# Order of the steps in the first pass of the second attention: variance before the score products on VectorE, ScalarE counted one tile later

## The chip, the cores and the metric

The kernel runs on one core of one Trainium2 chip. The metric is the device time of one execution in microseconds (us); the time of the kernel is the median of its runs.

## What is computed

The reference is four residual graph layers over 50000 nodes of 256 features and 12500 edges, each followed by a row norm. The change lies in the third layer, an attention with 8 heads over the edges, and there in what is computed per edge before the softmax:

```python
q = (nfeat @ Wq.T).reshape(n, HEADS, HEAD_DIM) / SCALING
k = (nfeat @ Wk.T).reshape(n, HEADS, HEAD_DIM)
v = (nfeat @ Wv.T).reshape(n, HEADS, HEAD_DIM)
attn = jnp.einsum('ehd,ehd->eh', k[src], q[dst]) + attn_bias
...
x = _layernorm(x + _L2_gnn_ref(...))
```

## The kernel before

The 12500 edges, sorted by destination, are 100 tiles of 125 edges. `attention_scores` (line 1864) is one pass over these tiles. It takes for each edge the row of its destination and the row of its source out of a table in HBM, brings the destination row to the norm that the layer before left open, projects both, and leaves two things in SBUF: V (the projected source row) and the score of each head. A barrier stands before the pass and after it; behind it come the maximum per destination and the sums.

Per tile, five queues work on it, each in an order that is written out by hand:

- POOL, `fetch`: two indirect gathers, the destination rows `xd` (a ring of 4 buffers) and the source rows `xs` (a ring of 8). It waits until ScalarE has normed the tile four earlier, whose `xd` buffer it fills again.
- VectorE: `stats` and `aggregate` (mean and variance of each row of `xd`), `variance` (two instructions on one column: `q`, line 1999, and `mean`, line 2001), `rest` (line 2006, the part of a transposed tile that rounding dropped), and `dots` (lines 2012 to 2014: product of k and q, sum per head, bias; after each of the three VectorE waits until it is done, and then counts `s_dot` up).
- ScalarE: `normed` (lines 1946 to 1951: logarithm, exponential, shift, and the normed rows `xn`), `copy_rows` (line 1957, the transposed tile out of PSUM, rounded), `copy_out` (lines 1963 and 1964: q scaled, and V, both out of PSUM).
- TensorE: `turn_rows` (line 1924, four transposes) and `project` (line 1935, 18 matmuls: q, k, v). A tile's `project` waits for its own `rest`, and, as its two PSUM buffers turn over, for `dots` and the copy of V two tiles earlier.
- SP: `keep` stores the normed rows.

The order on an engine is a list of (lag, step) pairs. `run_stages` (line 909) goes through the tiles t and runs, in the order of the list, each step on tile t - lag:

```python
for a in range(unroll):
    for lag, step in steps:
        step(At(turn, unroll, a - lag))
```

The first 16 passes and those behind pass 96 are written out with constant semaphore values (the head and the tail). The 80 passes between are a loop of eight passes per turn, in which semaphore values and addresses come from registers. Before, VectorE's list is `[(0, stats), (3, rest), (0, aggregate), (4, dots), (0, variance)]` and ScalarE's `[(0, normed), (1, copy_rows), (3, copy_out)]`. POOL has no loop: its 100 fetches are written out.

Of the kernel before, what the change touches and what calls it, by code (L numbers as in the profile page):

```python
# [36 lines left out]
T = E // P  # L37
# [39 lines left out]
class Chain:  # L77
# [5 lines left out]
    def step(self, ins):  # L83
        self.go(ins)
        self.done()
# [814 lines left out]
def wait(eng, sem, value):  # L900

    if not (isinstance(value, int) and value <= 0):
        eng.wait_ge(sem, value)
# [5 lines left out]
def run_stages(eng, steps, total, tiles=100, unroll=RING, behind=4):  # L909

    most = max(lag for lag, _ in steps)
    head = unroll * -(-(most + behind) // unroll)
    for t in range(head):
        for lag, step in steps:
            if 0 <= t - lag < total:
                step(At(0, unroll, t - lag))
    with eng.Fori(head // unroll, tiles // unroll) as turn:
# [3 lines that stand above are left out]
    for t in range(unroll * (tiles // unroll), total + most):  # L921
        for lag, step in steps:
            if 0 <= t - lag < total:
                step(At(0, unroll, t - lag))
# [939 lines left out]
def attention_scores(nc, env, V, score):  # L1864
# [10 lines left out]
    stages = dict(unroll=LONG, behind=LONG)  # L1875
# [11 lines left out]
    with nc.Block() as block:  # L1887
        @block.gpsimd
        def _(pool):
            dram = Rows(ph, pool, N)  # L1890
            pool.wait_ge(s_index, 4)

            def fetch(at):
                s, l = at.slot(RING), at.slot(LONG)
                wait(pool, s_st, at.count(1, 1 - RING))
                wait(pool, s_xn[s], at.uses(RING))
                wait(pool, s_t, at.count(1, 1 - LONG))
                dram.gather(xd[:, s, :], env["XX"], dst2[:, at.col], s_d[s])
                dram.gather(xs[:, l, :], env["XX"], src2[:, at.col], s_s[l])
            run_unrolled(pool, [(0, fetch)], T)  # L1900
# [39 lines left out]
        @block.scalar  # L1940
        def _(act):
            def normed(at):
                s = at.slot(RING)
                act.wait_ge(s_q, at.count(2, 2))
                ch = Chain(act, ca, at.count(3))
                ch.step(act.activation(lnq[:, s, :], q[:, s, :], ACT.Ln, bias=rec[:, at.col, 3]))
                ch.step(act.activation(c[:, s, :], lnq[:, s, :], ACT.Exp, scale=-0.5))
                ch.step(act.activation(nm[:, s, :], mean[:, s, :], ACT.Copy, scale=c[:, s, :]))
                wait(act, s_t, at.count(1, 1 - RING))
                wait(act, s_o[s], at.uses(RING, 32))  # L1950
                act.activation(xn[:, s, :], xd[:, s, :], ACT.Identity, bias=nm[:, s, :], scale=c[:, s, :]).then_inc(s_xn[s], 1)

            def copy_rows(at):
                s, b = at.slot(RING), at.slot(2)
                act.wait_ge(s_t, at.count(1, 1))
                wait(act, s_p, at.count(1, 1 - RING))
                act.copy(xT[:, s, 0, :, :], tp[:, b, :, 0:P]).then_inc(s_xT, 1)

            def copy_out(at):
                s, b = at.slot(RING), at.slot(2)  # L1960
                act.wait_ge(s_p, at.count(1, 1))
                wait(act, s_dot, at.count(1, 1 - RING))
                act.mul(qs[:, s, :], kq[:, b, F:2 * F], float(C2) ** 0.5).then_inc(s_qs, 1)
                act.copy(V[:, at.col, :].rearrange("p o f -> p (o f)"), vp[:, b, 0:F]).then_inc(s_V, 1)
            run_stages(act, [(0, normed), (1, copy_rows), (3, copy_out)], T, **stages)

        @block.vector
        def _(dve):
            dve.tensor_scalar(fresh[:, :], rec[:, :, 3], -1.0, 1.0, ALU.mult, ALU.add).then_inc(s_index, 1)
            dve.tensor_scalar(unfresh[:, :], rec[:, :, 3], 1.0, None, ALU.subtract).then_inc(s_index, 1)  # L1970
            dve.scalar_tensor_tensor(out=dst2[:, :], in0=rec[:, :, 3], scalar=float(N), in1=rec[:, :, 1],
                                     op0=ALU.mult, op1=ALU.add).then_inc(s_index, 1)
            dve.tensor_scalar(src2[:, :], rec[:, :, 0], float(N), None, ALU.add).then_inc(s_index, 1)
            dve.wait_ge(s_index, 2)
            weights = ((0, 2 * F, env["w_kv"]), (2 * F, 3 * F, env["w_q"]))
            for a, e, w in weights:
                dve.tensor_copy(wp[:, 0, :, a:e], w[:, :, :]).then_inc(s_wr, 1)
            dve.wait_ge(s_wr, 2)
            for a, e, w in weights:
                dve.tensor_tensor(wp[:, 1, :, a:e], w[:, :, :], wp[:, 0, :, a:e], ALU.subtract).then_inc(s_wp, 1)  # L1980

            def stats(at):
                s = at.slot(RING)
                dve.wait_ge(s_d[s], at.uses(RING, 16, 16))
                wait(dve, s_mv, at.count(1, 1 - RING))
                dve.bn_stats(st[:, s, :], xd[:, s, :]).then_inc(s_st, 1)

            def aggregate(at):
                s = at.slot(RING)
                wait(dve, s_q, at.count(2, 2 - 2 * RING))  # L1990
                dve.wait_ge(s_st, at.count(1, 1))
                dve.sem_inc(s_hold, 1)
                dve.bn_aggr(mv[:, s, :], st[:, s, :]).then_inc(s_mv, 1)

            def variance(at):
                s = at.slot(RING)
                dve.wait_ge(s_mv, at.count(1, 1))
                wait(dve, s_xn[s], at.uses(RING))
                dve.scalar_tensor_tensor(out=q[:, s, :], in0=mv[:, s, 1:2], scalar=EPS, in1=fresh[:, at.col],
                                         op0=ALU.add, op1=ALU.mult).then_inc(s_q, 1)  # L2000
                dve.tensor_scalar(mean[:, s, :], mv[:, s, 0:1], unfresh[:, at.col], None, ALU.mult).then_inc(s_q, 1)

            def rest(at):
                s, b = at.slot(RING), at.slot(2)
                dve.wait_ge(s_xT, at.count(1, 1))
                dve.tensor_tensor(xT[:, s, 1, :, :], tp[:, b, :, 0:P], xT[:, s, 0, :, :], ALU.subtract).then_inc(s_rest, 1)  # L2006

            def dots(at):
                s, b = at.slot(RING), at.slot(2)
                ch = Chain(dve, c1, at.count(3))  # L2010
                dve.wait_ge(s_qs, at.count(1, 1))
                ch.step(dve.tensor_tensor(prod[:, s, :], kq[:, b, 0:F], qs[:, s, :], ALU.mult))
                ch.step(dve.tensor_reduce(dot[:, s, :], prod[:, s, :].rearrange("p (h c) -> p h c", h=H2), X, ALU.add))
                ch.step(dve.tensor_tensor(score[:, at.col, :].rearrange("p o h -> p (o h)"), dot[:, s, :],
                                          rec[:, at.col, 4:4 + H2].rearrange("p o h -> p (o h)"), ALU.add))
                dve.sem_inc(s_dot, 1)
            run_stages(dve, [(0, stats), (3, rest), (0, aggregate), (4, dots), (0, variance)], T, **stages)
    ph.end()


# [515 lines left out]
```

## Time and profile before

| | us |
|---|---|
| median of 3 runs | 4572.68 |
| lowest and highest run | 4570.46, 4578.47 |
| the profiled execution, its own time | 4575.74 |
| its span in the trace | 4573.1 |
| first gather of the pass to the first instruction behind it | 3228.25 to 3673.60 |

The span is what the trace shows from the first to the last instruction. Over the whole program TensorE is busy for 75% of it, VectorE for 71%, POOL for 64% and ScalarE for 59%, but the program is a row of stages with a barrier between them, and a share over all of them tells nothing of one. The pass of this case is 445 us long, and it is read by itself: start times in a timeline are in us from the span's start, the second number is the duration in us, and what stands in square brackets at the end of a row is how long the engine was idle before it and which instruction ended that. A start that comes before the end of the row ahead on the same engine means that the two overlap.

### The profile page before, as it was taken

What the parts mean: (1) busy time and instruction counts of PE and PEld (TensorE: products, weight loads), DVE (VectorE), ACT (ScalarE), POOL (GpSimd) and SP (SyncE); (2) the same over time, 40 slices, a digit from 0 to 9 for tenths busy, and PEclk for the clock granted to TensorE, in tenths of its full rate; (3) what the DMA queues carried; (4) which work ended last, traced back from release to release, by engine and by line L of the source; (5) the groups of instructions that cost most, each with busy time, mean ns of one, the idle gap of its engine ahead of it and who ended that gap; (6) DMA issues with size and microseconds to landing.
All of it is one profiled execution on the core that took longest, in us unless ns stands there. A gap on an engine that the chain in (4) does not pass through costs nothing. (4 is left out here: it accounts for less than half of the span.)

```text
span 4573.1 us, 92084 instructions
## 1 busy us (share of the span) xinstructions
PE 3430.6 (75%) x17524; PEld 2595.8 (57%) x17524; DVE 3237.9 (71%) x11747; ACT 2715.4 (59%) x6436; POOL 2914.7 (64%) x2826
## 2 busy tenths in 40 slices
PE   4899934445999997999999777777566658850588
PEld 2799922223888886666666555555466635530365
DVE  7788843334555556999999798999555587740798
ACT  0688812222666666989989588888555536640366
POOL 0366658885434443888888788887655537667476
PEclk9999955555999998999999787777799979985799
DMA  1688823332444446888888333333333337753344
GB/s 54 177 237 236 238 74 80 79 80 79 162 161 161 161 161 185 269 268 267 264 265 267 104 99 99 98 100 97 98 88 88 86 95 213 214 161 82 97 135 115
DMA packets 437548, 685.41 MB, mean 150 GB/s; under 512 B 171062, under 2 KB 284588, under 8 KB 437396
## 3 DMA queue, kind: packets, MB, share of 16 engines
q1 hardware_dynamic: 263572, 521.77, 37.2%
q0 software_dynamic: 173824, 162.17, 14.7%
q14 instruction: 124, 1.02, 0.1%
q8 instruction: 28, 0.46, 0.0%
HBM read 352.28 MB, written 339.16 MB: 151 GB/s over the span
## 5 line engine op out<-in xcount | busy, mean ns | idle before, releaser
L1097 POOL TENSOR_TENSOR mlp_r_parts<-mlp_r,mlp_r_parts 128x500 fp32r<-128x500 f32 x200 | 253.0, 1265 | 403.4 <-ACT mlp_r_parts L1083 394.3
L1238 PE MATMUL nodes_xp<-w_self,nodes_x3T 128*125 128x256 f32 x1600 | 444.0, 400 | 45.5 <-DVE nodes_elu L1346 45.5
L791 PE MATMUL gram<-gin_both,gin_am 125*128 125x257 f32 x404 | 205.8, 665 | 266.8 <-DVE gin_both L774 254.6
L1238 PEld LDWEIGHTS nodes_xp<-w_self,nodes_x3T 128*125 128x125 f32 x1600 | 268.3, 187 | 111.3 <-ACT nodes_x3T L1277 39.0
L791 PEld LDWEIGHTS gram<-gin_both,gin_am 125*128 125x128 f32 x404 | 118.1, 322 | 354.4 <-issue 323.2
L1122 DVE BATCH_NORM_STATS2 mlp_stats<-mlp_y 128x500 f32 (+1 forms) x200 | 136.3, 682 | 253.3 <-ACT mlp_y L1073 253.3
L179 POOL DMA_INDIRECT by_src<-rank_recs,rank_place x100 | 119.7, 1197 | 293.2 <-DVE rank_recs L512 292.6
L1392 POOL TENSOR_TENSOR nodes_v<-nodes_elu,nodes_x 125x512 f32<-125x512 f32 x200 | 253.4, 1267 | 79.1 <-ACT nodes_x L1270 44.6
L1036 PE MATMUL mlp_y<-mlp_hT,mlp_w 128*128 128x500 f32 x1200 | 296.6, 396 | 1.5 <-DVE mlp_hT L1113 0.8
L1036 PE MATMUL mlp_y<-mlp_r_parts,mlp_w 128*128 128x500 f32 x1200 | 287.4, 388 | 0.8 <-ACT mlp_y L1073 0.8
L572 PE MATMUL gram<-rank_xc 125*128 125x257 f32 (+1 forms) x1600 | 279.1, 328 | 0.0
L1935 PE MATMUL att_kq<-att_w_parts,att_xT 128*125 128x256 f32 x1200 | 176.0, 298 | 136.6 <-DVE att_xT L2006 136.6
L572 PEld LDWEIGHTS gram<-rank_xc 125*128 125x128 f32 x1600 | 249.2, 191 | 22.4
L1081 ACT ACTIVATE mlp_r<-mlp_y,affine 128x500 f32<-128x500 f32 x200 | 153.7, 768 | 178.9 <-PE mlp_y L1036 178.9
L1036 PEld LDWEIGHTS mlp_y<-mlp_r_parts,mlp_w 128*128 128x128 f32 x1200 | 225.3, 188 | 47.1 <-POOL mlp_r_parts L1097 1.1
L744 DVE SCALAR_TENSOR_TENSOR gin_acc<-gin_acc,same,gin_msg 125x256 f32<-125x256 f32 x100 | 48.4, 484 | 286.6 <-ACT gin_msg L716 205.7
L1384 POOL TENSOR_SCALAR nodes_x<-nodes_u,nodes_r,nodes_nm 125x256 f32<-125x256 f32 x400 | 217.7, 553 | 45.7 <-DVE nodes_nm L1339 33.9
L1935 PEld LDWEIGHTS att_kq<-att_w_parts,att_xT 128*125 128x125 f32 x1200 | 154.7, 194 | 158.8 <-DVE att_xT L2006 138.6
L1036 PEld LDWEIGHTS mlp_y<-mlp_hT,mlp_w 128*128 128x128 f32 x1200 | 218.1, 188 | 41.0 <-DVE mlp_hT L1116 1.1
L716 ACT ACTIVATE gin_msg<-gin_xd,srec 125x256 f32<-125x256 f32 x100 | 50.7, 507 | 316.0 <-DMA gin_xd<-x,other 316.0
L1251 ACT ACTIVATE nodes_z<-nodes_y,affine 128x250 f32<-128x250 f32 x400 | 215.2, 588 | 33.3 <-ACT nodes_r L801 18.0
L175 POOL DMA_INDIRECT att_xd<-XX,att_dst x100 | 121.4, 1214 | 159.0 <-issue 150.5
(426 smaller groups left out, 11951.3 us busy)
## 6 DMA issues: line engine op xcount, KB each, us to landing
XX<-mlp_y SPq DMA_DIRECT2D x100, 500.0 KB
nodes_y<-XX SPq DMA_DIRECT2D x100, 500.0 KB
rank_xin<-x SPq DMA_DIRECT2D x100, 448.0 KB
XP<-rank_xc SPq DMA_DIRECT2D x100, 448.0 KB
mlp_h<-XP SPq DMA_DIRECT2D x100, 448.0 KB
nodes_x<-x SPq DMA_DIRECT2D x100, 448.0 KB
XX<-nodes_x SPq DMA_DIRECT2D x100, 448.0 KB
out<-nodes_out SPq DMA_DIRECT2D x100, 448.0 KB
```

Source lines behind the costliest of these rows:

```text
L175: self.pool.indirect_dma_start(out, None, table, bass.IndirectOffsetOnAxis(index, 0)).then_inc(sem, 16)
L572: mm = pe.matmul(gram[:, m, 128 * m:F + 1], xc[:, s, j, 128 * m:128 * m + 128], xc[:, s, j, 128 * m:F + 1], start=False, stop=True, skip_g ...
L791: mm = pe.matmul(gram[:, m, 0:F + 1], am[:, s, 128 * m:128 * m + 128], both[:, s, 0:F + 1], start=False, stop=True, skip_group_check=True)
L1036: mm = pe.matmul(out[:, m, 0:CH], w[:, a, k, 128 * m:128 * m + 128], rows[:, s, b, k, :], start=((k, a, b) == terms[0]), stop=((k, a, b) = ...
L1081: act.activation(r[:, s, m, :], y1[:, m, 0:CH], ACT.Relu, bias=aff[:, 1, m:m + 1], scale=aff[:, 0, m:m + 1]).then_inc(s_r, 1)
L1097: pool.tensor_tensor(rp[:, s, 1, m, :], r[:, s, m, :], rp[:, s, 0, m, :], ALU.subtract).then_inc(s_rp, 1)
L1122: dve.bn_stats(stats[:, m, at.col, :].rearrange("p o n -> p (o n)"), y[:, s, m, :]).then_inc(s_st, 1)
L1238: pe.matmul(xp[:, b, j, :], x3T[:, s, k, P * j:P * j + P], w_self[:, k, 0:F], start=(k == 0), stop=False)
L1251: act.activation(z[:, s, m, :], y[:, c, m, HC * h:HC * h + HC], ACT.Relu, bias=aff[:, 3, m:m + 1], scale=aff[:, 2, m:m + 1]).then_inc(s_z, 1)
L1384: pool.tensor_scalar(x1[:, s, j, :], u[:, at.slot(LONG), j, :], r[:, s, 0, j:j + 1], nm[:, s, 0, j:j + 1], ALU.mult, ALU.add).then_inc(s_x ...
L1392: pool.tensor_tensor(v[:, at.slot(LONG), :, :], el[:, s, :, :], x3[:, at.slot(LONG), :, :], ALU.add).then_inc(s_v, 1)
L1935: mm = pe.matmul(out, xT[:, s, i, x0 + k, :], wp[:, j, k, w0:w0 + F], start=((k, i, j) == terms[0]), stop=((k, i, j) == terms[-1]), skip_g ...
```

## The change

```diff
@@ attention_scores, block.scalar
-            run_stages(act, [(0, normed), (1, copy_rows), (3, copy_out)], T, **stages)
+            run_stages(act, [(1, normed), (2, copy_rows), (4, copy_out)], T, **stages)
@@ attention_scores, block.vector
-            run_stages(dve, [(0, stats), (3, rest), (0, aggregate), (4, dots), (0, variance)], T, **stages)
+            run_stages(dve, [(0, stats), (3, rest), (0, aggregate), (0, variance), (5, dots)], T, **stages)
```

On VectorE, pass t now does `variance` of tile t right behind `aggregate` of tile t, and only then `dots`, of tile t - 5 in place of t - 4. On ScalarE all three lags are one higher. No instruction is added, removed or changed in shape; PE, POOL and SP have the same rows in the same order.

VectorE in the loop, from `rest` on, in the kernel before (q and mean are `variance`, prod, dot and score are `dots`; ISA and REGISTER_ALU rows are waits and register work between the instructions):

```order
L2006 TENSOR_TENSOR att_xT<-att_tp,att_xT 128x500
L1991 REGISTER_ALU
L1993 BN_AGGR att_mv<-att_stats 125x2
L2012 TENSOR_TENSOR att_prod<-att_kq,att_qs 125x256
L93 REGISTER_ALU
L2013 TENSOR_REDUCE att_dot<-att_prod 125x8
L93 REGISTER_ALU
L2014 ISA
L2014 REGISTER_ALU
L2014 TENSOR_TENSOR att_score<-att_dot,srec 125x8
L1999 ISA
L1999 SCALAR_TENSOR_TENSOR att_q<-att_mv,att_fresh 125x1
```

and the same place in the kernel with the change:

```order
L2006 TENSOR_TENSOR att_xT<-att_tp,att_xT 128x500
L1991 REGISTER_ALU
L1993 BN_AGGR att_mv<-att_stats 125x2
L1999 ISA
L1999 SCALAR_TENSOR_TENSOR att_q<-att_mv,att_fresh 125x1
L2001 REGISTER_ALU
L2001 TENSOR_SCALAR att_mean<-att_mv,att_unfresh 125x1
L2012 TENSOR_TENSOR att_prod<-att_kq,att_qs 125x256
L93 REGISTER_ALU
L2013 TENSOR_REDUCE att_dot<-att_prod 125x8
L93 REGISTER_ALU
L2014 ISA
```

`variance` has moved from behind `dots` to ahead of it; what stands behind the score's row there (not shown) is the next pass's `stats`.

ScalarE just ahead of the loop's branch (line 917), one piece of the difference:

```order
 L1963 ACTIVATE att_qs<-att_kq 125x256
 L1964 COPY att_v<-att_vp 125x256
-L1946 ACTIVATE att_lnq<-att_q,srec 125x1
-L1947 ACTIVATE att_c<-att_lnq 125x1
-L1948 ACTIVATE att_nm<-att_mean,att_c 125x1
-L1951 ACTIVATE att_xn<-att_xd,att_nm,att_c 125x256
-L1957 CAST att_xT<-att_tp 128x500
-L1963 ACTIVATE att_qs<-att_kq 125x256
-L1964 COPY att_v<-att_vp 125x256
 L917 UNCONDITIONAL_BRANCH
```

The same seven rows stand behind the loop's end in the kernel with the change. Since all three lags rise by the same one, the order of ScalarE's work by tiles (`normed` of tile m, `copy_rows` of m - 1, `copy_out` of m - 3) is the order of before, and only the place where head, loop and tail are cut has moved by one tile.

## Rows read from the trace of the kernel before

**Rows 1.** Windows: stretch, length; PE, PEld, DVE, ACT, POOL busy us (instructions); PEclk, DMA, GB/s.

```profile
3256.50:3295.40 38.90, 28.09 (x221) 25.77 (x220) 23.03 (x81) 23.97 (x71) 24.23 (x20) 1.00 0.40 100
3297.00:3650.00 353.00, 237.72 (x1758) 220.15 (x1759) 188.66 (x640) 192.00 (x560) 193.54 (x160) 0.96 0.34 88
2540.00:2900.00 360.00, 263.78 (x1071) 185.88 (x1070) 307.16 (x1371) 262.51 (x763) 286.79 (x246) 0.78 0.37 98
3243.10:3247.00 3.90, 3.88 (x18) 3.88 (x19) 1.43 (x6) 1.39 (x4) 2.99 (x4) 0.50 0.46 119
```

**Rows 2.** Waits from 3260 to 3660: engine, line, releaser: total us, times, longest.

```profile
ACT att_lnq L1946 <- DVE att_mean L2001: 168.1, 92, 2.0
```

**Rows 3.** Timeline, one tile in the loop, DVE, ACT and POOL.

```profile
3451.79 0.18 DVE L1999 SCALAR_TENSOR_TENSOR att_q<-att_mv,att_fresh 125x1 f32<-125x1 f32 x1 [0.33 <-DVE att_score L2014]
3451.90 0.21 DVE L2001 TENSOR_SCALAR att_mean<-att_mv,att_unfresh 125x1 f32<-125x1 f32 x1
...
3452.27 0.29 ACT L1946 ACTIVATE att_lnq<-att_q,srec 125x1 f32<-125x1 f32 x1 [1.89 <-DVE att_mean L2001]
...
3453.16 0.60 ACT L1951 ACTIVATE att_xn<-att_xd,att_nm,att_c 125x256 f32<-125x256 f32 x1
3453.67 0.55 ACT L1957 CAST att_xT<-att_tp 128x500 fp32r<-128x500 f32 x1
3454.12 0.38 ACT L1963 ACTIVATE att_qs<-att_kq 125x256 f32<-125x256 f32 x1
...
3454.54 0.42 DVE L2012 TENSOR_TENSOR att_prod<-att_kq,att_qs 125x256 f32<-125x256 f32 x1 [1.37 <-ACT att_qs L1963]
3454.64 1.21 POOL L175 DMA_INDIRECT att_xd<-XX,att_dst  x1 [1.66 <-issue]
...
3455.69 0.17 DVE L2014 TENSOR_TENSOR att_score<-att_dot,srec 125x8 f32 x1 [0.27 <-DVE att_dot L2013]
...
3456.20 0.16 DVE L1999 SCALAR_TENSOR_TENSOR att_q<-att_mv,att_fresh 125x1 f32<-125x1 f32 x1 [0.34 <-DVE att_score L2014]
```

**Rows 4.** The same timeline going on, DVE and PE.

```profile
3456.44 0.42 DVE L1986 BATCH_NORM_STATS2 att_stats<-att_xd 125x6 f32<-125x256 f32 x1
...
3456.77 0.66 DVE L2006 TENSOR_TENSOR att_xT<-att_tp,att_xT 128x500 fp32r<-128x500 f32 x1
...
3457.35 0.17 DVE L1993 BATCH_NORM_AGGREGATE att_mv<-att_stats 125x2 f32<-125x6 f32 x1
...
3457.49 1.67 PE L1935 MATMUL att_kq<-att_w_parts,att_xT 128*125 128x256 f32 x12 [1.53 <-DVE att_xT L2006]
...
3459.71 0.38 PE L1924 MATMUL att_tp<-ident,att_xs 125*128 125x125 f32 x2
...
3459.93 0.38 PE L1924 MATMUL att_tp<-ident,att_xn 125*128 125x125 f32 x2
```

**Rows 5.** Timeline of the pass's start, POOL, DVE and PE.

```profile
3228.25 1.42 POOL L175 DMA_INDIRECT att_xd<-XX,att_dst  x1 [8.48 <-DVE att_src L1973]
...
3234.57 1.21 POOL L175 DMA_INDIRECT att_xd<-XX,att_dst  x1 [0.30 <-issue]
...
3239.26 0.43 DVE L1986 BATCH_NORM_STATS2 att_stats<-att_xd 125x6 f32<-125x256 f32 x1 [2.64 <-DMA att_xd<-XX,att_dst]
3239.83 0.18 DVE L1993 BATCH_NORM_AGGREGATE att_mv<-att_stats 125x2 f32<-125x6 f32 x1
3240.05 0.16 DVE L1999 SCALAR_TENSOR_TENSOR att_q<-att_mv,att_fresh 125x1 f32<-125x1 f32 x1
...
3243.12 2.92 PE L1935 MATMUL att_kq<-att_w_parts,att_xT 128*125 128x256 f32 x12 [3.83 <-DVE att_xT L2006]
...
3247.13 0.39 PE L1924 MATMUL att_tp<-ident,att_xs 125*128 125x125 f32 x2
```

**Rows 6.** Timeline of the pass's last tiles, DVE.

```profile
3665.43 0.17 DVE L2014 TENSOR_TENSOR att_score<-att_dot,srec 125x8 f32<-125x8 f32 x1
...
3665.74 0.68 DVE L2006 TENSOR_TENSOR att_xT<-att_tp,att_xT 128x500 fp32r<-128x500 f32 x1 [0.15 <-DVE att_score L2014]
```

## The prediction, made blind

> **What bounds the pass now.** I read the windows first, for the rate. In the loop POOL issues 160 gathers in 353 us, two per tile: 80 tiles at 4.41 us each. In the head, where nothing comes from registers, it is 20 gathers in 38.9 us, 3.89 per tile [rows 1]. No engine is full: per tile of the loop TensorE is busy for 237.72 / 80 = 2.97 us, VectorE 2.36, ScalarE 2.40, POOL 2.42 [rows 1]. So the period is a ring of waits, not a load. Then the waits: ScalarE idles 168.1 us over 92 tiles, 1.83 each, until VectorE's `mean` is there [rows 2], and a timeline of one tile closes the ring [rows 3]: q starts at 3451.79, mean 0.11 later, ScalarE's logarithm 0.37 after that, its copy of the transposed tile 1.40 later, the scaled q 0.45 later, VectorE's product 0.42 after that (it had idled 1.37 for it), the score 1.15 later, and the next q 0.51 behind the score, at 3456.20. Sum 4.41, the whole period. VectorE and ScalarE hand one tile's work to and fro and each waits while the other works. `variance` needs nothing from `dots`; it is late only because it stands behind it.
>
> **What the change does to that ring.** VectorE's order is opened: q now follows `aggregate`, and `dots` comes after. ScalarE's part alone does nothing: all three lags rise by one, so its steps keep their order and only the cut between head, loop and tail moves; I cost it at 0. I cost VectorE's move at 0 busy time too, as no instruction is added. The old ring still exists, but runs over three tiles: from a q, 2.75 to the product, then 1.15 to the score, and some 1.66 through stats, rest and aggregate to a q, which is that of three tiles later: 5.6 / 3 = 1.9 per tile. It no longer decides. Four things can be next.
>
> 1. *VectorE by itself*, start to start: stats to rest 0.33, rest to aggregate 0.58 [rows 4]; q to what follows mean 0.24 [rows 3, 4]; product to score 1.15 [rows 3]. Two steps are not in the trace of the loop. Aggregate to q: 0.22 in the head [rows 5], and at most the loop's 0.51 from score to q, which has one register row more [rows 3]; I take 0.36, the middle. Score to stats: 0.31 is the tail's score to rest [rows 6], 0.51 again the upper end; I take 0.39, nearer the tail, as no register write for an address stands there. Sum 0.33 + 0.58 + 0.36 + 0.24 + 1.15 + 0.39 = 3.05; ends 2.83 and 3.32.
>
> 2. *A ring over two tiles through TensorE.* `project` of tile m waits for `dots` of m - 2, and `dots` of m stands behind `rest` of m + 2. From the start of q, k, v to the end of the next transposes 2.82 (3457.49 to 3460.31) [rows 4]; to ScalarE 0.04, as from scaled q to product [rows 3]; its copy 0.55 [rows 3]; 0.04 to VectorE; rest to aggregate 0.58; aggregate to q 0.36; to product 0.24; to score 1.15; score 0.17, its completion 0.14 [rows 6], the signal to TensorE 0.06 as from rest to the matmul [rows 4]. Sum 6.15, per tile 3.08. With the ends of aggregate to q, 3.00 and 3.15.
>
> 3. *POOL*: a gather takes 1.21 and stands 0.30 behind the one ahead [rows 5], two per tile are 3.02.
>
> 4. *The gather's ring of four buffers.* The gather of tile m + 4 starts 0.88 after the norm of m ends (3453.76 to 3454.64) [rows 3]; with 1.21 and a landing 3.48 behind it (3235.78 to 3239.26) [rows 5] it is 5.6 to stats. From stats to the end of the norm: 0.91 to aggregate, 0.36, 0.11 and 0.37 to the logarithm, 1.49 to the end of xn [rows 3, 4], 3.2. Together 8.8 over four tiles, 2.2 per tile. The stores of xn have the same four periods. Not the bound.
>
> Three limits lie within 2% of each other: 3.02, 3.05, 3.08. Where several nearly tie, a delay in one is seldom made up by the others, so I take 3.13 for the loop.
>
> **The sum**, against the profiled execution's 4575.74 us (span 4573.1), which is 3.1 above the median of the runs. Loop: 80 x (4.41 - 3.13) = 102. Head: some 10 tiles at 3.89 [rows 1] go to POOL's 3.02: 9. Tail: 3 such tiles: 3. After the last q one more `dots` than before has to be done, 1.15 + 0.39 and its waits: 2 back. In all 112 us, 4464 for that execution, 4461 for a run like the median; I say 4462. The barrier behind the pass means that the later stages just start earlier. If both open steps of VectorE are at their low ends, POOL's 3.02 rules: 80 x 1.39 + 9 + 3 - 2 = 121, some 4451. At their high ends, 3.32: 80 x 1.09 + 10 = 97, some 4475.
>
> What TensorE costs is hidden only while its own step stays under 3.08: its busy 2.97 leaves little. If the cover goes, ring 2 grows by half of whatever `project` and the transposes grow by.
>
> [...] The very first gather took 1.42, while VectorE was still rounding the weights; later ones 1.21 [rows 5]. If the denser VectorE made every gather 1.42, POOL's step would be 2 x 1.72 = 3.44. [...]
>
> **Rivals.**
> - *VectorE's own issue is dearer than its rows say* (register work after each wait is not hidden once the engine no longer idles): 3.32 to 3.6. For it: the same steps take 0.5 us more per tile in the loop than in the head [rows 1]. Against: I have put the loop's values in wherever there are any. 4475 to 80 x 0.81 + 10 = 75, some 4498.
> - *POOL slowed by VectorE*, 3.44: 80 x 0.97 + 6 = 84, some 4489. For: the first gather. Against: the loop's 1.21 beside a VectorE that works for half of the time.
> - *TensorE at the low clock, and slower than before.* In the window from 3243.10 the granted clock was 0.50, the 1.2 GHz level, after an idle of 3.83 [rows 1, 5], and there from the start of `project` to the transposes it took 4.01 (3243.12 to 3247.13), against 2.22 at full clock [rows 4, 5], 1.81 times. TensorE's own step, 2.82 to the end of the transposes, would be 5.10. Then the loop takes 80 x 0.69 = 55 more, the head 10 x 1.21 = 12 more: some 4640. It decides from 70% of the tiles at the low level, where (1 - s) x 2.82 + s x 5.10 passes 4.41. For it: an earlier stage with TensorE busy for 73% of the time has a mean clock of 0.78 [rows 1]. Against: this loop has 0.96, with longer idle between tiles (1.53 [rows 4]) than it will have. The Trainium skill, TensorE: Matmul & The Clock Gate, section What's actually happening, says that the low level is the default and that activity releases it; by that the change makes it rarer.
> - *At a mean clock like that stage's 0.78*, s is 44%, and with 3.13 for the others the loop's tile takes some 4.0: 80 x 0.41 + 5 = 38, some 4535.
> - *No effect*: if the gathers' landing or the stores set 4.41, the opened ring would be filled by another wait. Against: the same gathers run at 3.89 in the head, and POOL's first ones at 3.02 with landings of at most 3.48 [rows 1, 5]. 4573.
>
> **Chances.** The forecast (3.02 to 3.32, 4451 to 4475) 0.72; dearer issue 0.16; POOL slowed 0.04; mean clock of 0.78 0.02; no effect 0.02; slower by the clock or by a wait that I don't see 0.04. Range 4450 to 4494: the forecast, most of the dearer issue, and POOL slowed; the rest, about one in ten, is left out. The measurement tells about 0.2%, 9 us, from no change: faster by more 0.94, within it 0.02, slower 0.04.
>
> **What would show it.** Right: ScalarE's wait for mean and VectorE's for the scaled q nearly gone from the waits; q right behind aggregate; POOL's gathers per window at 3.0 to 3.2 us per tile; TensorE's idle ahead of `project` from 1.5 to some 0.3, ended by VectorE; gathers still 1.21; later stages of unchanged length. Step 1 is wrong if aggregate to q or score to stats lies outside 0.22 to 0.51 and 0.31 to 0.51; step 2 if TensorE starts `project` without having waited; step 4 if stats waits for a gather in the loop. The forecast is wrong if the loop's period is above 3.32.

## The result, and the profile after

The kernel with the change takes 4454.23 us (median of 4 runs, 4452.22 to 4457.48) against 4571.57 us for the kernel before in the runs beside it (4567.44 to 4578.47): a ratio of 0.9742, with a 95% interval of 0.9727 to 0.9756. That is 117 us less. 4462 was forecast, with a range of 4450 to 4494. One of all the executions reported here, of the kernel with ScalarE's part alone, was a slow one (7072.83 us), and the times and ratios leave it out.

In the profiled execution (4455.06 us, span 4452.6) the pass runs from its first gather at 3229.52 to the first instruction behind it at 3555.56: 326.0 us in place of 445.4. What lies behind it takes 897.0 us in place of 899.5. So nearly all of the gain, 119.3 us of 120.5 in the span, is in this pass.

The windows of the changed kernel, head and loop, with the columns of [rows 1]:

```profile
3260.00:3290.00 30.00, 26.27 (x211) 24.62 (x210) 22.21 (x77) 22.84 (x66) 24.12 (x20) 1.00 0.50 129
3290.00:3530.00 240.00, 216.97 (x1706) 201.03 (x1705) 182.96 (x621) 187.35 (x544) 187.77 (x156) 1.00 0.49 125
```

One tile is 22 matmuls, so the loop's 1706 are 77.5 tiles in 240 us: 3.10 per tile, where it was 4.41. The head's 20 gathers in 30 us are 3.0 per tile, where they were 3.89. In the loop TensorE's granted clock is 1.00, the full 2.4 GHz, all the time, where it was 0.96. A gather still takes 187.77 / 156 = 1.20 us, though VectorE is now busy for 76% of the loop.

The waits of the changed kernel from 3260 to 3540:

```profile
ACT att_xT L1957 <- PE att_tp L1924: 50.5, 89, 1.5
...
PE att_kq L1935 <- issue: 24.7, 76, 1.2
DVE att_stats L1986 <- DVE att_score L2014: 24.1, 85, 0.8
...
DVE att_stats L1986 <- DMA att_xd<-XX,att_dst: 4.8, 6, 1.6
```

ScalarE's wait for `mean`, 168.1 us before [rows 2], is not among them any more. Nor is VectorE's wait for the scaled q, which in the kernel before was this, from 3260 to 3660:

```profile
DVE att_prod L2012 <- ACT att_qs L1963: 126.8, 92, 1.6
```

What is left is small and spread: 0.57 per tile on ScalarE until the transposes are done, 0.3 of TensorE ahead of `project`, and 0.28 of VectorE behind the score, which is mostly its own completion. The six waits of stats for a landing are all in the head, before 3290; in the loop there is none.

The timeline of one tile of the loop, DVE, PE, ACT and POOL; it answers to [rows 3, 4]:

```profile
3400.80 0.17 DVE L2014 TENSOR_TENSOR att_score<-att_dot,srec 125x8 f32 x1 [0.26 <-DVE att_dot L2013]
...
3401.12 1.66 PE L1935 MATMUL att_kq<-att_w_parts,att_xT 128*125 128x256 f32 x12 [0.19 <-issue]
3401.18 0.43 DVE L1986 BATCH_NORM_STATS2 att_stats<-att_xd 125x6 f32<-125x256 f32 x1 [0.21 <-DVE att_score L2014]
3401.32 1.21 POOL L175 DMA_INDIRECT att_xd<-XX,att_dst  x1 [0.38 <-issue]
...
3401.58 0.68 DVE L2006 TENSOR_TENSOR att_xT<-att_tp,att_xT 128x500 fp32r<-128x500 f32 x1
...
3401.97 0.32 ACT L1946 ACTIVATE att_lnq<-att_q,srec 125x1 f32<-125x1 f32 x1
3402.18 0.17 DVE L1993 BATCH_NORM_AGGREGATE att_mv<-att_stats 125x2 f32<-125x6 f32 x1
...
3402.48 0.16 DVE L1999 SCALAR_TENSOR_TENSOR att_q<-att_mv,att_fresh 125x1 f32<-125x1 f32 x1
...
3402.72 0.41 DVE L2012 TENSOR_TENSOR att_prod<-att_kq,att_qs 125x256 f32<-125x256 f32 x1
...
3403.55 0.38 PE L1924 MATMUL att_tp<-ident,att_xn 125*128 125x125 f32 x2
3403.86 0.17 DVE L2014 TENSOR_TENSOR att_score<-att_dot,srec 125x8 f32 x1 [0.27 <-DVE att_dot L2013]
3403.96 0.58 ACT L1957 CAST att_xT<-att_tp 128x500 fp32r<-128x500 f32 x1 [0.48 <-PE att_tp L1924]
...
3404.19 1.65 PE L1935 MATMUL att_kq<-att_w_parts,att_xT 128*125 128x256 f32 x12 [0.26 <-issue]
...
3404.61 0.66 DVE L2006 TENSOR_TENSOR att_xT<-att_tp,att_xT 128x500 fp32r<-128x500 f32 x1
...
3407.19 1.65 PE L1935 MATMUL att_kq<-att_w_parts,att_xT 128*125 128x256 f32 x12 [0.22 <-issue]
...
3407.74 0.43 DVE L1986 BATCH_NORM_STATS2 att_stats<-att_xd 125x6 f32<-125x256 f32 x1 [0.70 <-DVE att_score L2014]
```

On VectorE q (3402.48) now stands 0.30 behind aggregate, and the product follows it 0.24 later without a wait, as the scaled q was ready. VectorE goes round in 3.08 (3401.18 to the next stats at 3404.26, which is the row 0.40 behind the score at 3403.86). Both ends of TensorE's ring are there: `project` starts 0.15 behind the score's end (3400.80 + 0.17 to 3401.12) and not at the end of a `rest`; the transposes end at 3403.93, the copy starts at 3403.96, rest at 3404.61, and the `project` that closes the ring over two tiles starts at 3407.19: 6.07. At 3407.74 stats has idled 0.70 in place of 0.21: there the loop's branch stands.

### The profile page after: what moved, and what is told of

It reads as the page before. It is cut to its first block and busy times, and to the rows that moved or that the text cites. A ratio compares the mean times of both kernels' runs of the same rounds, so it can differ in the third digit from the quotient of the medians.

```text
span 4452.6 us, 92084 instructions
## 1 busy us (share of the span) xinstructions
PE 3421.2 (77%) x17524; PEld 2592.3 (58%) x17524; DVE 3237.9 (73%) x11747; ACT 2716.9 (61%) x6436; POOL 2920.4 (66%) x2826
## 5 line engine op out<-in xcount | busy, mean ns | idle before, releaser
L1399 POOL TENSOR_SCALAR nodes_out<-nodes_v,nodes_r,nodes_nm 125x256 f32<-125x256 f32 x400 | 220.4, 560 | 1.1 <-DMA out<-nodes_out 1.1
L1270 ACT ACTIVATE nodes_x<-nodes_u,nodes_nm,nodes_r 125x256 f32<-125x256 f32 x400 | 219.1, 599 | 0.0
```

What stands on the lines that cost most here:

```text
L1270: act.activation(x3[:, at.slot(LONG), j, :], u[:, at.slot(LONG), j, :], ACT.Identity, bias=nm[:, s, 1, j:j + 1], scale=r[:, s, 1, j:j + 1] ...
L1399: pool.tensor_scalar(out[:, s, j, :], v[:, l, j, :], r2[:, l, j:j + 1], nm2[:, l, j:j + 1], ALU.mult, ALU.add).then_inc(s_out, 1)
```

## Experiments

Two theories were set against each other in the first four kernels. Mine: one ring over one tile was opened by VectorE's part alone, and other limits near 3.05 took over. The rivals: that ScalarE's lag belongs to it, that the place of `variance` is what counts, or that the distance of `dots` is. All edits are to the two lists in `attention_scores`.

### VectorE's part alone, ScalarE's part alone

VectorE's part alone:

```diff
-            run_stages(dve, [(0, stats), (3, rest), (0, aggregate), (4, dots), (0, variance)], T, **stages)
+            run_stages(dve, [(0, stats), (3, rest), (0, aggregate), (0, variance), (5, dots)], T, **stages)
```

> VectorE's list as in the change, ScalarE's lags as before (0, 1, 3). Theory: ScalarE's order by tiles is the same with either lags, so this is the change itself: 4452 to 4458 us, a loop of 3.10 per tile. Rival, that ScalarE's extra tile of distance is part of the gain: between 4480 and 4572.

ScalarE's part alone:

```diff
-            run_stages(act, [(0, normed), (1, copy_rows), (3, copy_out)], T, **stages)
+            run_stages(act, [(1, normed), (2, copy_rows), (4, copy_out)], T, **stages)
```

> ScalarE's lags as in the change (1, 2, 4), VectorE's list as before. Theory: nothing moves but the cut between head, loop and tail: 4567 to 4578 us, a loop of 4.41 per tile. Rival, that the lag on ScalarE opens the ring by itself: 4454.

Measured: VectorE's part alone 4457.45 us against 4576.47 for the kernel before on the same chip, ratio 0.974 (0.9724 to 0.9756), the ratio of the whole change. ScalarE's part alone took 4576.92 (median of nine runs), ratio 1.0001 (0.9991 to 1.0011). The windows of the two loops, first VectorE's part alone:

```profile
3290.00:3530.00 240.00, 216.35 (x1702) 200.45 (x1701) 182.49 (x618) 186.38 (x542) 188.02 (x156) 1.00 0.49 125
```

and ScalarE's part alone:

```profile
3297.00:3650.00 353.00, 230.58 (x1759) 212.62 (x1757) 188.15 (x639) 191.59 (x559) 193.95 (x160) 0.98 0.34 88
```

1702 matmuls in 240 us are 3.10 per tile, 1759 in 353 us are 4.41. Of the two lines of the diff, only VectorE's does anything. The lags of an engine among themselves set its order, and the run shows for ScalarE that a constant added to all of them moves nothing.

### The order without the extra tile

```diff
-            run_stages(dve, [(0, stats), (3, rest), (0, aggregate), (4, dots), (0, variance)], T, **stages)
+            run_stages(dve, [(0, stats), (3, rest), (0, aggregate), (0, variance), (4, dots)], T, **stages)
```

> Variance ahead of the score products as in the change, but these keep their lag of 4. Theory: the one-tile ring is open all the same. What is left is a ring over two tiles, rest 0.66, 0.06, project to the end of the next transposes 2.82, 0.04, copy to scaled q 0.45, 0.39, 0.04, product to score 1.15, score to stats 0.39, stats to rest 0.33: 6.33, or 3.17 per tile against 3.10 in the change: 4458 to 4466 us. Rival A, the extra tile of distance of the score products is what counts: 4572. Rival B, POOL's gathers bound the loop now at 3.03: 4450 to 4456.

Measured: 4469.67 us, ratio 0.9764 (0.9748 to 0.978); the kernel before took 4576.47 on that chip, so beside the first runs' 4571.57 this would be 4464. Rivals A and B are both out: most of the gain is there, and not all. The loop's window:

```profile
3290.00:3530.00 240.00, 206.51 (x1613) 190.07 (x1613) 175.96 (x588) 180.23 (x513) 179.23 (x148) 1.00 0.47 119
```

1613 matmuls are 73.3 tiles, 3.27 per tile where 3.17 was expected. The timeline shows what was right and what was left out. Three of its rows around the loop's branch:

```profile
3384.13 0.66 DVE L2006 TENSOR_TENSOR att_xT<-att_tp,att_xT 128x500 fp32r<-128x500 f32 x1
...
3387.55 0.43 DVE L1986 BATCH_NORM_STATS2 att_stats<-att_xd 125x6 f32<-125x256 f32 x1 [0.71 <-DVE att_score L2014]
...
3387.89 0.66 DVE L2006 TENSOR_TENSOR att_xT<-att_tp,att_xT 128x500 fp32r<-128x500 f32 x1
```

and five behind it:

```profile
3390.97 0.66 DVE L2006 TENSOR_TENSOR att_xT<-att_tp,att_xT 128x500 fp32r<-128x500 f32 x1
...
3394.32 0.66 DVE L2006 TENSOR_TENSOR att_xT<-att_tp,att_xT 128x500 fp32r<-128x500 f32 x1
...
3395.27 1.65 PE L1935 MATMUL att_kq<-att_w_parts,att_xT 128*125 128x256 f32 x12 [0.77 <-DVE att_xT L2006]
...
3396.96 0.43 DVE L1986 BATCH_NORM_STATS2 att_stats<-att_xd 125x6 f32<-125x256 f32 x1 [0.21 <-DVE att_score L2014]
3397.30 0.66 DVE L2006 TENSOR_TENSOR att_xT<-att_tp,att_xT 128x500 fp32r<-128x500 f32 x1
```

From one `rest` to the next but one it is 3390.97 to 3397.30, 6.33, the ring's sum to the hundredth. But from 3384.13 to 3390.97 it is 6.84: between them stats has idled 0.71 in place of 0.21 at VectorE's branch. And at 3395.27 `project` starts 0.29 behind the end of a rest (3394.98) where it was 0.06. It is the first `project` of a turn of TensorE's loop, and every eighth one is late by as much: TensorE pays at its own branch. My sum had no term for the turn of the loop, and on this ring, which has no slack, both turns are paid: 0.51 on VectorE and 0.23 on TensorE, once in eight tiles.

### The extra tile without the order

```diff
-            run_stages(dve, [(0, stats), (3, rest), (0, aggregate), (4, dots), (0, variance)], T, **stages)
+            run_stages(dve, [(0, stats), (3, rest), (0, aggregate), (5, dots), (0, variance)], T, **stages)
```

> The score products one tile later (lag 5), but still ahead of the variance, as before the change. Theory: the scaled q that they wait for now comes from the ScalarE pass before, so the old ring runs over two tiles, 4.41 / 2 = 2.2, and VectorE alone and POOL bound the loop at 3.03 to 3.10: 4450 to 4456 us. Rival, the place of the variance is what counts: 4572.

Measured: 4449.78 us, ratio 0.9719 (0.9702 to 0.9735). The old ring is open here too, though `variance` still stands behind `dots`: the place of `variance` is not what counts. The loop's window, the waits from 3260 to 3540, and four gathers on POOL:

```profile
3290.00:3530.00 240.00, 221.64 (x1745) 205.36 (x1744) 180.21 (x633) 192.53 (x555) 191.82 (x159) 1.00 0.50 127
```

```profile
POOL att_xs L175 <- issue: 27.8, 91, 0.3
POOL att_xd L175 <- issue: 26.5, 87, 0.3
...
DVE att_stats L1986 <- DMA att_xd<-XX,att_dst: 13.4, 36, 1.0
```

```profile
3402.14 1.22 POOL L175 DMA_INDIRECT att_xs<-XX,att_src  x1 [0.30 <-issue]
...
3403.66 1.21 POOL L175 DMA_INDIRECT att_xd<-XX,att_dst  x1 [0.30 <-issue]
...
3405.18 1.21 POOL L175 DMA_INDIRECT att_xs<-XX,att_src  x1 [0.30 <-issue]
...
3406.69 1.21 POOL L175 DMA_INDIRECT att_xd<-XX,att_dst  x1 [0.30 <-issue]
```

1745 matmuls are 79.3 tiles, 3.03 per tile. POOL's gathers stand 0.30 apart everywhere, 1.52 from start to start, and stats now waits for a landing 36 times in this stretch, where it did 6 times with the change, and never in the loop. POOL is the bound here, at the 3.02 of [rows 5].

### One tile too far

If the ring through TensorE is real, a sixth tile of distance must close it over one tile, and the kernel must fall behind the one before, with no work added.

```diff
-            run_stages(dve, [(0, stats), (3, rest), (0, aggregate), (0, variance), (5, dots)], T, **stages)
+            run_stages(dve, [(0, stats), (3, rest), (0, aggregate), (0, variance), (6, dots)], T, **stages)
```

> As the change, with the score products one tile later still (lag 6). Theory of the ring through TensorE: project of tile m waits for the score products of m - 2, and with lag 6 these stand behind rest of m + 1, whose transposes stand behind project of m - 1. The same 6.15 us that the change pays over two tiles are then paid over one: some 6.15 per tile in the loop against 3.10, 5.7 in head and tail, 4455 + 80 x 3.05 + 45: 4720 to 4770 us, slower than before. Rival, that VectorE and POOL alone bound the change at 3.0 to 3.1 and TensorE's ring has room: 4450 to 4465.

Measured: 4905.96 us, ratio 1.0725 (1.0706 to 1.0745). The direction and the mechanism are as the theory has them; the size is not: the loss against the change, which took 4452.59 on the same chip, is 453 us where some 290 were expected. The loop's window, and one tile of it:

```profile
3390.00:3590.00 200.00, 117.71 (x555) 111.30 (x555) 61.02 (x200) 60.30 (x175) 61.09 (x52) 0.65 0.19 48
```

```profile
3507.72 0.17 DVE L2014 TENSOR_TENSOR att_score<-att_dot,srec 125x8 f32 x1 [0.26 <-DVE att_dot L2013]
...
3508.04 2.89 PE L1935 MATMUL att_kq<-att_w_parts,att_xT 128*125 128x256 f32 x12 [3.34 <-issue]
...
3512.01 0.62 PE L1924 MATMUL att_tp<-ident,att_xs 125*128 125x125 f32 x2
...
3512.43 0.42 PE L1924 MATMUL att_tp<-ident,att_xn 125*128 125x125 f32 x2
3512.88 0.57 ACT L1957 CAST att_xT<-att_tp 128x500 fp32r<-128x500 f32 x1 [5.63 <-PE att_tp L1924]
...
3513.49 0.68 DVE L2006 TENSOR_TENSOR att_xT<-att_tp,att_xT 128x500 fp32r<-128x500 f32 x1 [4.96 <-ACT att_xT L1957]
...
3515.77 0.17 DVE L2014 TENSOR_TENSOR att_score<-att_dot,srec 125x8 f32 x1 [0.27 <-DVE att_dot L2013]
...
3516.10 2.89 PE L1935 MATMUL att_kq<-att_w_parts,att_xT 128*125 128x256 f32 x12 [3.25 <-issue]
```

555 matmuls in 200 us are 25.2 tiles, 7.9 each. From `project` at 3508.04 to the next at 3516.10 it is 8.06, and each link waits for the one ahead: the transposes' end at 3512.85, the copy at 3512.88, rest at 3513.49, the score at 3515.77, `project` 0.33 behind it. Without TensorE's part the sum is 3.25, against 3.33 in the forecast of ring 2 (6.15 less 2.82). TensorE's part is 4.81 (3508.04 to 3512.85) in place of 2.82, as the granted clock has a mean of 0.65 in this loop: TensorE idles 3.3 us ahead of each `project` shown, and the matmuls of both then start at the low level. From 3508.00 to 3510.90 and from 3516.10 to 3519.00 the granted clock is 0.50, which is 1.2 GHz, and q and k take 2.89 in place of 1.65.

### The version with the lag alone, against the change

> The change itself, as the measure on this chip for the version with the lag alone: a ratio of 0.974 to the kernel before, a loop of 3.10 per tile, one step of eight longer by 0.5 at the loop's branch.

> The lag of 5 alone, variance behind the score products. Theory: in the first run POOL's gathers bound it at 3.04 per tile with nothing left for the loop's branch; so it beats the change by 80 x 0.06 = 5 us, a ratio of 0.9725 to 0.9735 to the kernel before. Rival: the earlier 0.9719 was a chip's luck, and both are the same within 2 us.

Measured, on one chip: the change 4452.59 us (4446.28 to 4454.13), ratio 0.9732 (0.9719 to 0.9745); the lag alone 4443.66 us (4440.05 to 4446.84), ratio 0.9717 (0.9704 to 0.9731). The kernel before took 4573.96. The change came out as expected. The lag alone is ahead by 9 us in the medians, where 5 were expected; the two intervals still overlap, and the fastest run of the change (4446.28) lies within those of the lag alone. On the chip of the first four kernels it was ahead of VectorE's part alone, which is the change in all that counts, by 8 us, so luck with a chip is unlikely. In the profiled executions the pass itself takes 325.8 (3224.37 to 3550.17) and 319.4 (3221.29 to 3540.72), 6.4 us less, and that is the part which the order can explain.

The cause of the 6.4 is argued from the trace, not tested by itself. With `dots` ahead of `variance` TensorE's ring does not carry the steps over q: the product starts 0.09 behind aggregate, where the change has 0.54 (3402.18 to 3402.72), so the ring of 6.1 is shorter by 0.45. From the first run of the lag alone:

```profile
3402.69 0.17 DVE L1993 BATCH_NORM_AGGREGATE att_mv<-att_stats 125x2 f32<-125x6 f32 x1
3402.78 0.39 DVE L2012 TENSOR_TENSOR att_prod<-att_kq,att_qs 125x256 f32<-125x256 f32 x1
```

VectorE's own round is shorter too: between two stats it takes as little as 2.84, and in the change never under 2.97. This slack can take up the turn of the loop, and POOL's gathers are never more than 0.3 apart. Of the versions that ran it has the lowest median on both chips.

## Why the prediction was right

- **What bounded the pass, and what opened it.** Right: the ring of one tile with its sum of 4.41 was the bound. It is open in each kernel in which q no longer stands behind a product that waits for the norm of the tile just ahead (the change, VectorE's part alone, the order alone, the lag alone), and as closed as before with ScalarE's part alone.
- **ScalarE's part at 0.** Right, 1.0001.
- **VectorE by itself, 3.05.** The two steps that the trace of before did not have came out at 0.30 for aggregate to q (0.39 in about one pass of four; 0.36 taken, between 0.22 and 0.51) and 0.38 for score to stats (0.39 taken). The step goes round in 3.08 where it also waits for ScalarE's copy.
- **The ring through TensorE, 3.08.** 6.07 over two tiles in the change where 6.15 was summed. The kernel with lag 6, where it closes over one tile, shows it as a ring.
- **POOL at 3.02.** Right, and seen pure in the lag alone. Between the loop's turns the change is held by VectorE, TensorE's ring or POOL, which lie within some 2% of each other; no run separates the first two.
- **The gather's ring, 2.2.** Not the bound: with the change stats never waits for a landing in the loop.
- **The loop at 3.13.** It is 3.10. The 0.05 that I added to 3.08 for near ties stood in for something else: eight tiles are 24.8, of which the loop's branch takes 0.49 of VectorE (0.70 less 0.21), so the other steps are at 3.04, near POOL's limit. That 3.13 came so near is luck: the margin had the size of a cost that the sum left out. The loop gave 80 x 1.31 = 105 us in place of 102.
- **The sum.** The pass gave 119.3 us where 112 was forecast. Split by VectorE's stats, the head (first gather to the stats of the 17th tile) went from 64.9 to 53.6, 11 in place of 9; the 80 passes of the loop from 353.4 to 248.4, 105 in place of 102; tail and drain from 27.1 to 24.0, 3 in place of 1.
- **The rivals.** Dearer issue: no, the steps cost what their rows said. POOL slowed by VectorE: no, gathers still take 1.20 beside a VectorE that is busy for 76% of the time. The Trainium skill (SBUF — State Buffer, Who interferes with whom) says that a VectorE instruction with at most one SBUF input, outside the modes that use two ports, does not contend with GpSimd. The trace agrees as far as it goes: of the long operations `rest` and the product read their other input from PSUM, and the gathers did not slow. TensorE at the low clock: not in the change, whose clock is 1.00. It came with lag 6, not from more work but from longer idling. The Trainium skill (TensorE: Matmul & The Clock Gate, What's actually happening) says that the low level is the default and that activity releases it, and both agree with it.

One check of the prediction was badly put: that TensorE's idle ahead of `project` would be ended by VectorE. The trace gives "issue" for 76 of these waits; that VectorE's count of finished `dots` ends them is read from the times, 0.15 behind the score's end, and from the kernel with lag 6.

## What to carry to other kernels

When two engines hand a tile to and fro and each idles for nearly half of its period, add up one ring of waits from row to row. If the sum is the period, look for a step that stands on the ring only by its place in an order: here a new order and lag, with no instruction made faster, took the pass from 445 to 326 us. Then sum the rings over two tiles and the engines alone before choosing the lag: here 4, 5 and 6 tiles gave 0.976, 0.973 and 1.07, and a lag longer by one tile may close a ring through a double buffer elsewhere. A constant added to every lag of one engine changed nothing here, and the change of lag by itself came out some 0.2% ahead of the change of order and lag together.

## What was not expected of the hardware

TensorE's clock fell far with lag 6: the mean granted clock is 0.65 in a loop with some 3.3 us of idle ahead of each `project`. It was 0.96 in the kernel before, with some 1.5 us ahead of most and 2.0 once in eight tiles, and 1.00 in the change, with 0.2 to 0.4 and 0.8 once in eight tiles. So the ring of 6.15 became one of 8.0: a wait on TensorE cost not only its own length but 2 us more in slower matmuls. And the turn of a loop of registers is not free on VectorE: in the change and in the order alone it idles 0.70 to 0.75 ahead of the first stats of a turn, once in eight tiles, against 0.21 to 0.30 elsewhere.
